# Second attention: products with the values in two blocks a pair of heads instead of five

## The reference, cut to what matters

```
q = (layernorm(x) @ wq_w + wq_b)          # 16 heads of 64
k = concat(ctx @ wk_w + wk_b, mk)         # 512 keys of the context + 128 of a memory = 640
v = concat(ctx @ wv_w + wv_b, mv)
attn = softmax(q @ k.T / sqrt(64))        # per head, 512 x 640
x = x + (attn @ v) @ wo_w + wo_b
```

## Time and profile before

| | us |
|---|---|
| median of 3 runs | 1897.2 |
| the profiled execution's own time | 1897.06 |
| its span (first to last instruction) | 1895.4 |
| second attention, about | 985 to 1700 of the span |
| TensorE busy in the whole span | 1528.2 (81%) |
| VectorE busy | 983.6 (52%) |
| ScalarE busy | 520.2 (27%) |
| GpSimd busy | 461.1 (24%) |
| mean granted TensorE clock | 0.914 |

### The profile page before, as it was taken

How to read it: one execution, slowest core, us unless ns; L and a number is a source line. 1 busy time by engine, 2 the same in 40 slices (tenths; PEclk the granted TensorE clock), 3 DMA queues, 4 the chain that set the end, 5 groups by cost and what they waited for, 6 DMA issues and landing times. The chain is left out here.

```text
span 1895.4 us, 19508 instructions
## 1 busy us (share of the span) xinstructions
PE 1528.2 (81%) x6124; PEld 898.5 (47%) x6152; DVE 983.6 (52%) x1690; ACT 520.2 (27%) x683; POOL 461.1 (24%) x261
## 2 busy tenths in 40 slices
PE   2788888889864999960589988999799979995996
PEld 1333434334353777750244445444544444444785
DVE  5556565565540000012257773777468746765666
ACT  0233332333401222210133331433133314340221
POOL 3000000000023000023025451444244433372333
PEclk9789999999966999985789998999899989996898
DMA  5602321122025555514745552565265526502001
GB/s 135 141 21 27 44 34 20 25 34 34 1 85 202 174 175 175 175 37 91 99 59 76 79 68 34 71 87 78 27 81 78 67 34 84 78 6 91 1 1 45
DMA packets 61467, 136.07 MB, mean 72 GB/s; under 512 B 9825, under 2 KB 20449, under 8 KB 56801
## 3 DMA queue, kind: packets, MB, share of 16 engines
q1 hardware_dynamic: 58672, 127.26, 36.3%
q0 software_dynamic: 2736, 8.13, 1.2%
HBM read 58.55 MB, written 12.06 MB: 37 GB/s over the span
## 5 line engine op out<-in xcount | busy, mean ns | idle before, releaser
L1250 POOL TENSOR_TENSOR a_probs<-a_probs 128x1024 f32<-128x1024 f32 x128 | 305.2, 2384 | 495.2 <-PE a_p_o L1587 494.3
L1291 ACT ACTIVATE a_probs<-a_p_s 128x1024 f32<-128x1024 f32 x160 | 164.0, 1025 | 324.9 <-PE a_p_s L1573 324.9
L407 DVE CUSTOM_DVE_ANT_0 a_scratch<-a_p_m,a_bias_q 128x512 bf16<-128x512 f32 x256 | 171.7, 690 | 119.5 <-PE a_p_m L560 115.4
L1392 DVE TENSOR_REDUCE a_max_ctx<-a_p_m 128x1 f32<-128x512 f32 x256 | 169.1, 687 | 61.2 <-PE a_p_m L1548 57.8
L320 ACT ACTIVATE a_probs<-a_p_s 128x1024 f32<-128x1024 f32 x128 | 130.6, 1025 | 195.6 <-PE a_p_s L585 188.6
L560 PE MATMUL a_p_m<-a_k_stack,a_q_stack 127*128 127x512 f32 x256 | 127.8, 529 | 40.4 <-DVE a_mx L407 20.7
L1384 DVE TENSOR_TENSOR a_lo<-a_full,a_hi 128x512 fp32r<-128x512 f32 x64 | 91.7, 1433 | 129.0 <-ACT a_hi L1280 129.0
L1587 PE MATMUL a_p_o<-a_probs,a_v 128*64 128x512 f32 x512 | 138.1, 618 | 0.0
L1004 PE MATMUL e_p_h<-e_rows_t,e_w 128*128 128x256 f32 x480 | 122.5, 389 | 13.9 <-DVE e_rows_t L942 13.9
L1548 PE MATMUL a_p_m<-a_k_hl,a_q_hh 128*128 128x512 f32 x256 | 110.2, 471 | 27.4 <-DVE a_max_ctx L1392 15.8
L583 PE MATMUL a_p_s<-a_q_stack,a_k_stack 128*128 128x512 f32 x256 | 118.9, 491 | 10.9 <-DMA a_q_stack<-a_neg_max 10.9
(11 more groups left out here) (196 smaller groups left out, 2322.2 us busy)
## 6 DMA issues: line engine op xcount, KB each, us to landing
e_w<-in_L_w SPq DMA_DIRECT2D x30, 1024.0 KB
a_q_hh<-a_hi SPq DMA_DIRECT2D x64, 256.0 KB, 4.9
a_q_lm<-a_lo SPq DMA_DIRECT2D x32, 256.0 KB, 6.9
a_k_hl<-a_hi SPq DMA_DIRECT2D x32, 256.0 KB, 5.7
a_k_hl<-a_lo SPq DMA_DIRECT2D x32, 256.0 KB, 7.2
a_k_h<-a_hi SPq DMA_DIRECT2D x32, 256.0 KB, 8.2
a_ctx_t<-in_ctx_t SPq DMA_DIRECT2D x8, 512.0 KB, 4.1
a_q_stack<-a_hi SPq DMA_DIRECT2D x16, 256.0 KB, 6.2
```

Of the source, the lines that this page charges most:

```text
L407: dve.tensor_tensor_reduce(scratch[:, fill.n % 2, :], m, bias_q[:, i % NT, :], 1.0, -3.0e38, ALU.add, ALU.max, mx[:, i:i + 1]).then_inc(m_ ...
L1250: pool.tensor_tensor(probs[:, kt], probs[:, kt - 1], probs[:, kt], ALU.add)\
L1291: act.activation(probs[:, kt, :, :], p_s[:, (KT1 * p + kt) % 2, :, :], ACT.Exp).then_inc(exp_done.sem, 1)
L1392: dve.tensor_reduce(max_ctx[:, NT * head + t:NT * head + t + 1], m, AX, ALU.max)\
```

## The change

`times_v` disappears from rows 1, 2 and 4 of `STEPS`. In row 3 the word now stands for tiles 0, 1 and 2 of this pair, one after the other; in row 0 for tiles 3 and 4 of the pair before. The second `value` moves behind the first maximum of row 1, and the other `value` ahead of two maxima in row 2; the number of maxima in each row stays. `normalize` is now taken by VectorE at the word `total`.

```
-                 ("score", "score", "value", "maximum", "maximum", "times_v", "maximum"),
-                 ("maximum", "score", "score", "maximum", "value", "times_v", "maximum"),
+                 ("score", "score", "maximum", "value", "maximum", "maximum"),
+                 ("maximum", "score", "score", "value", "maximum", "maximum"),
                  ("maximum", "score", "score", "maximum", "times_v", "maximum", "rows"),
-                 ("maximum", "total", "score", "score", "times_v", "turn"))
+                 ("maximum", "total", "score", "score", "turn"))
+        PV_FIRST = 3
...
-                            if what == "times_v" and kt == 4 and p:
+                            if what == "total" and p:
                                 normalize(b, p - 1)
...
                             elif what == "times_v" and kt:
-                                times_v(b, p, kt - 1)
+                                for k in range(PV_FIRST):
+                                    times_v(b, p, k)
                             elif what == "times_v" and p:
-                                times_v(b, p - 1, KT1 - 1)
+                                for k in range(PV_FIRST, KT1):
+                                    times_v(b, p - 1, k)
...
-                times_v(b, PAIRS - 1, KT1 - 1)
+                for k in range(PV_FIRST, KT1):
+                    times_v(b, PAIRS - 1, k)
```

## The result

| us | before | changed | difference |
|---|---|---|---|
| median (4 runs each, beside each other) | 1897.01 (1894.03 to 1899.41) | 1990.1 (1989.82 to 1994.62) | +93 |
| span of the profiled execution | 1895.4 | 1988.2 | +92.8 |
| TensorE busy in the span | 1528.2 | 1545.4 | +17.2 |
| mean granted TensorE clock | 0.914 | 0.907 | |

The ratio is 1.0497, 95% interval 1.0476 to 1.0518: slower, as forecast, but by 93 us where the sum said 70. 1990 lies 6 us above the top of the range.

The account below looks back on a forecast made before the run. TensorE was taken to set the pace up to `total`, VectorE from there to the key projection. +41, +31, -4 and +2 made +70 us on 1897.06: 1967, own range 1950 to 1984, whole range 1907 to 1984.

Parts of the forecast that it names:

- K: Start of a pair's key projection on TensorE; K to `total` was 13.70 us in an odd pair, forecast 15.05.
- second sum / join: After the block of three: GpSimd's second sum starts at 4.56, VectorE's join of the maxima at 4.59, 0.03 us behind.
- `total` to key: Stretch from `total` to the next key projection, limited by VectorE: +1.2 us in 26 stretches, +31 in all.
- pair 4: Join ends with the second sum anyway; the multiplication gains 1.03 there: -1 us in each of 4 elements.
- waits of maxima for the reductions: Sign that the forecast is right: TensorE's maxima wait over 30 us for VectorE's reductions, up from 15.
- low part of the keys: VectorE operation at K + 3.45: waits out GpSimd's third sum, then gets in ahead of the fourth; costed at nothing.
- first pair: Pair 0 of an element: the transpose behind the join waits as long as the reciprocal elsewhere, counted at +1.2 us.
- granted clock: TensorE's clock: a lower one in the longer stalls could add some; no size given.
- the case: Second sum starts before the join and has the port, so the join waits: 1967 us, chance 0.52.
- the walk: Step-by-step timing of a pair in the new order: K to `total` +1.35 us odd, +1.4 even, +41 over thirty pairs.
- The rival in which the join slips in first: Join gets the port before the second sum, -0.93 us a stretch; +19 in all, 1916 us, chance 0.34.
- TensorE's 33 us: Saved by merging products: 0.34 us a merger, three a pair, 32 pairs, if TensorE is the limit; not in the sum.

Follow-up runs that it names:

- e1: Changed kernel with the join made a reduction of one tile (one SBUF input) in place of an operation with two: 1934.81 us, ratio 1.0189.
- e5: Changed kernel with its own two-input join, GpSimd's second sum of each pair held until the join is done: 1936.62 us, ratio 1.0213.
- e10: Changed kernel with the one-input join and GpSimd's third sum held until VectorE has written the low part of the keys: 1908.18 us, ratio 1.0057.
- e6: Kernel before with GpSimd's fourth sum held until VectorE has written the low part of the keys: 1872.83 us, ratio 0.9884.
- e9: Changed kernel with one more fp32 matmul of 512 columns ahead of each transpose of the maxima, in the wait for the join: 1984.04 us, ratio 1.0479.
- e2: Kernel before with the one-input join: 1895.82 us, ratio 1.0000.
- e7: Kernel before with the one-input join, third sum held until the multiplication is done, fourth until the keys' low part is written: 1868.1 us, ratio 0.9855.

## Why the prediction was right, and where it fell short

| step | forecast | measured |
|---|---|---|
| block of two / of three | 1.87 / 2.73 | 1.86 / 2.72 |
| third maximum, first merger worth | K + 6.67, nothing | K + 6.67, nothing |
| seventh maximum: start, stall | K + 9.90, 0.7 | K + 9.89, 0.50 |
| `total`, odd / even | K + 15.05, +1.4 | K + 15.04, +1.44 |
| second sum / join, from the block's start X | 4.56 / 4.59 | 4.55 / 4.58 |
| join ends, reciprocal begins | X + 6.95, `total` + 3.33 | X + 6.93, `total` + 3.31 |
| multiplication | 0.69 | 0.69 |
| `total` to key | +1.2 | +1.16 |
| pair 4, `total` to key | -1 | 5.53 from 6.56, -1.03 |
| waits of maxima for the reductions | from 15 to over 30 | 23.5 from 15.2; with the `a_v` rows 36.6 from 23.5 |
| low part of the keys | gets in ahead of the fourth sum | it does (1268.63, the sum drawn out to 2.61) |
| first pair, last score matmul to transpose | +1.2 | +1.44 (2.78 from 1.34, from start to start) |
| granted clock | costed at nothing | about 19 us |
| sum | +70 | +93 |

**Right: the direction, its place and its size at the full clock.** The choice of the case rested on 0.03 us and on the one row; the trace has the same 0.03 and the engine that started first had the port. That the order came out right is partly luck: the walk was called good to 0.3 us a pair, ten times this margin, and the prediction gave the case 0.52. e1 and e5 show that it was the port: either taking it from the join or taking the sum out of its way returns 55 us. The rival in which the join slips in first would have left a join of 0.17. (Its sum left out the -1 us of pair 4 in each element; with it the rival stood at about 1912 and not 1916, and nothing else hangs on it.) The rule on the Trainium skill's page "SBUF — State Buffer", section "SBUF: two separate sides", that whichever engine starts first holds the shared port for its whole instruction, is borne out by this trace down to 0.03 us.

**Right: nothing is saved by merging.** The blocks are as short as forecast, so TensorE's 33 us are real, and none of them arrive. In e10, with the two collisions out of the way, the maxima still wait 28 us, where those of e6 wait 8. One sign was read from half of the view: 15 to over 30 us was meant for the reductions' rows, and these went to 23.5 only. The walk does not hang on it, as its starts (K + 9.89, K + 15.04) are where it put them.

**Failed: the term for the granted clock.** The prediction had it as a half sentence in the forecast's own range ("could add some") and its sum at the kernel before's clock, although that trace showed the clock low at the ends of elements, where TensorE waited. What it measured: four pairs of 2.74, 11.0; pair 5 of the last element, 4.4; the two first pairs, 1.5 and 2.5. Together about 19 of the 22 us by which the sum was short. At the end of the first element, where the clock is low in both kernels, another 1 us was lost (23.7 from the last `total` to the next query projection, 22.6 before). The range's top should have lain at about 2000: the lower level was in the trace, and one more stretch in a few pairs is 10 to 20 us.

**Failed, smaller: the first pairs.** They were sized like the others at +1.2. But the transpose waits for the join itself there: +1.44 in each of four elements, 1 us more in all. From key projection to transpose the four grew by 12.0 us together, where 4 x 2.58 = 10.3 was forecast.

**Open: when the clock falls.** In the one profile that each kernel has, those whose odd pairs have `total` at K + 15 (changed, e1, e5, e9) had stretches at 1.2 GHz between a key projection and its `total`, and those with 14.4 or less had none there. But e10 (14.37) had one in pair 5 of the last element, as had the changed kernel, e5 and e9, while e1 with the same order of work had none there. The pairs concerned were all odd ones; before the clock fell, TensorE had stood for 1.22 us before the third maximum (in the last element's pair 5 for 1.10) and had otherwise worked. But other odd pairs with the same stalls kept the full clock. e9, the one run on this question, filled another wait and didn't decide it.

## What to carry to other kernels

Before moving triggers of GpSimd work, write down when each operation takes the shared port and when VectorE's operations with two SBUF inputs come: a join that came 0.03 us behind a sum took 1.7 us longer, 26 times here. Such a collision has two cheap cures, an operation with one SBUF input or a wait on the less urgent engine, and the cure must reach the last collision of the chain, not the first (e2 against e7). Before gathering scattered work into a block to save its switches, ask what each piece covered where it stood: here a product between two uses of the two-bank ring fell into the time of a read, and in one block the products left the reads bare.

## What the runs showed of the hardware that was not expected

- Making GpSimd wait makes the kernel faster: e6 by 24 us and e7 by 29 us. In e6 a sum of 2.37 us starts 1.15 later (K + 4.23, from 3.08) and leaves the port to a VectorE operation of 0.69; no wait of TensorE in the pairs grew by it.
- The granted clock fell to the level of 1.2 GHz for 3.4 to 10 us at a time inside pairs in which TensorE is busy for 13.21 of 15.04 us at the full clock. The executions of one kernel differ with it: e9's lie 17 us apart, with mean clocks from 0.913 to 0.907, and e1's 16 us, with 0.911 to 0.902; e10's, with a single such stretch in its profile, lie 6 us apart.
- Shortening one operation of a chain by 0.5 us changed nothing at all when the next one met the same engine at the port (e2): the end of that one is set by the sum, not by its own start.
